# Routing product read from PSUM, row loads in quarters, line split ahead of the crosses, weight split and gate load moved

## Chip, cores and metric

The kernel runs on one core of a Trainium2 chip. The metric is the device time of one execution in microseconds, the median of several runs: 1242.65 us before the change (three runs, 1239.29 to 1244.85).

## What is computed

One transformer block on x of 32 batches x 256 tokens x 128 channels, in fp32. Six modulation vectors per batch come from c. Cut to what matters:

```
h = layernorm(x) * (1 + ca) + sa
q, k, v = h @ w_qkv.T + b_qkv                      # 16 heads of 8
write = exterior(h_prev @ w1_write.T, h @ w2_write.T)   # per head a unit 6-vector ("line")
read  = exterior(h @ w1_read.T, h @ w2_read.T)
logits = q k^T / sqrt(8) + (read . J write) * decay**(i-j) * [i>j] * bias_scale
x = x + ga * (softmax(causal logits) v @ w_out.T + b_out)
h = layernorm(x) * (1 + cb) + sb
top 2 of 8 experts by h @ Wg; weights p = softmax of the two logits
x = x + gb * sum_k p_k * ((silu(h W1[e]) * (h W2[e])) @ W3[e])
```

exterior(p1, p2) takes the six products p1[i] p2[j] - p1[j] p2[i] and divides them by their norm.

## The kernel before

**Attention stage (attend).** All engines run the same 40 iterations, b = -4 to 35, each of eight steps p = 0 to 7 (lines 101 to 104). Nothing synchronises the engines but semaphores; each has its own list of work by (b, p). In iteration b the attention of batch b is worked out, two heads per step, while the parts of other batches around it are in flight: normalisation and projections of b+3 and b+4, lines of b+2 and b+3, output projection of b-1, second norm and routing of b-2 and b-3. The small jobs that PE does between the heads stand in the table JOBS with their step, place and offset (lines 59 to 68).

A step on the engines: PE makes scores (L631 to L633) into the tile sc, incidences (L620) into inc, and for the next batch the prescores (L644 to L646) into pre; DVE weighs the incidences (L827), adds them to the scores (L794), and takes the maximum of the prescores (L806, with L811 after each four); ACT takes the exponentials (L1033); PE multiplies with the values (L660, L662). The prescores run one step less than a batch ahead: in step p of iteration b, for p from 1 on, they are those of pair p-1 of batch b+1 (lines 107 to 109).

**Rows.** fp32 numbers are cut into three bf16 parts. For the keys and queries ("dims") and for the lines, these parts are written to DRAM (kq_rows, by store_dims and store_lines: 6 and 12 DMAs by spread, L554) and read back in the layout of the scores: KT, QF, QI (load_rows, L579 to L581: three DMAs for a half of the heads). The maxima go the same way through POOL (split_peaks, L1189 to L1196), PE (L705), ACT (L1005) and a small DMA (load_peaks, L586). All these DMAs are issued by SP in one fixed order per iteration b (lines 588 to 600): peaks of b (second half), rows of b+1 (second half), store of the lines of b+2, peaks of b+1 (first half), rows of b+2 (first half), store of the dims of b+3. load_rows first holds for the stores of its batch. PE waits for the rows at the first prescores of each half (L640), so at steps 1 and 5 of an iteration.

**Lines, on POOL.** For batch b+3 at step 2: four outer products (L1236) and the cross differences (L1245, and three of L1247), then ACT squares them at step 4 (L1027), DVE sums them (L873), and at step 5 the norm is refined and applied (L1254 to L1264). For batch b+2: L1272, ACT's first part (L1061), the rest (L1128) at step 1, ACT's second part (L1064), and the last part (L1133) at step 3, behind the crosses; its end releases store_lines.

**Routing, batch b-3.** DVE marks the two chosen experts (L847, L854) at step 0. At step 2 PE's job "rank" (L738 to L741, three bf16 products) counts for each token the earlier ones with the same expert. At step 3 DVE adds the expert's base (L820, out of PSUM into slot_at), and after its maximum of the prescores it multiplies with the marks (L880, both operands in SBUF), takes the slot (L885), adds 1 to the exponential of the gap (L889), and works out the two weights (L891, L894). POOL then scatters the four token rows by indirect DMA (L1223, four per batch).

**Between the stages.** Behind its iterations ACT copies the weights' rounded parts into w_hi, which lies over the query tiles (L1112, 8 copies); DVE counts tiles per expert (L949 to L970) and subtracts to get w_lo (L974, 8 times); pads are written; then a barrier.

**Expert stage (experts).** 136 tiles of 128 tokens. SP loads a tile (L1358, up to 16 ahead), PE transposes it (L1377), multiplies up (L1384 to L1386), transposes (L1394) and multiplies down (L1402); ACT and DVE do silu, product and scaling; POOL scatters the result (L1542). ACT begins the stage with the load of gate_row (L1439, 2 MB) and a table load (L1441). The gates are used only in the last part, which adds both experts' results and x.

Of the kernel before, what the change touches and what calls it, by code (L numbers as in the profile page):

```python
# [412 lines left out]
def attend(nc, whole, stack, sb, sem, signal, v):  # L413
# [6 lines left out]
    with stack.enter_context(ExitStack()):  # L420
# [40 lines left out]
        slot_at = a("slot_at", [P, NT, E]); slot_pick = a("slot_pick", [P, NT, 2, E])  # L461
# [34 lines left out]
        rows_loaded = [signal(f"rows_loaded{n}", 48) for n in range(2)]  # L496
# [8 lines left out]
        route_step = signal("route_step", 6)  # L505
# [28 lines left out]
        with nc.Block() as block:  # L534
            @block.sync
            def _(sp):
# [33 lines left out]
                def load_rows(jb, par, half):  # L570

                    heads = slice(8 * half, 8 * half + 8)
                    hold(dims_stored, jb)
                    hold(lines_stored, jb)
                    hold(sc_ready, jb - 2, 4 * half + 4)
                    hold(inc_ready, jb - 2, 4 * half + 4)
                    hold(pre_ready, jb - 1, 4 * half + 1)
                    done = rows_loaded[half].sem
                    sp.dma_start(KT[par][0:TOP, heads, :], kq_rows[par][0, :, heads, :]).then_inc(done, 16)  # L579
                    sp.dma_start(QF[par][0:RAW0, heads, :], kq_rows[par][1, 0:RAW0, heads, :]).then_inc(done, 16)  # L580
                    sp.dma_start(QI[par][RAW0:TOP, heads, :], kq_rows[par][1, RAW0:TOP, heads, :]).then_inc(done, 16)  # L581
# [30 lines left out]
            def _(pe):  # L612
# [24 lines left out]
                def prescores(b, par, p):  # L637

                    if p % 4 == 0:
                        wait(pe, rows_loaded[p // 4], b)  # L640
# [25 lines left out]
                def job(n, b, par):  # L666
# [68 lines left out]
                    elif name == "rank":  # L735
# [4 lines left out]
                        nc.tensor.matmul(B[:, E:2 * E], onesb[:], hot_sum[:, 0, :], start=False, stop=False)  # L740
                        last = nc.tensor.matmul(B[:, 0:NT * E].rearrange("p (t e) -> p t e", t=NT), onesb[:],  # L741
# [43 lines left out]
            def _(dve):  # L785
                def body(b, par):
                    for p in range(8):
# [24 lines left out]
                        extras(b, par, p)  # L812

                def bank_copies(b, p):

                    if p == 3 and live(b - 3):
                        jb = b - 3
                        wait(dve, ready["rank"], jb)
                        B = bank[BANK["rank"]]
                        nc.vector.tensor_tensor(slot_at[:], B[:, 0:NT * E].rearrange("p (t e) -> p t e", t=NT),  # L820
                                                v["ebase"][:].unsqueeze(1).broadcast_to([P, NT, E]), ALU.add)\
                          .then_inc(used["rank"].sem, 1)
# [20 lines left out]
                def extras(b, par, p):  # L843
# [33 lines left out]
                    if p == 3 and live(b - 3):  # L877
                        jb, mine = b - 3, stage[1 - par]
                        wait(dve, used["rank"], jb)
                        nc.vector.tensor_tensor(slot_pick[:], hot[:],  # L880
                                                slot_at[:].unsqueeze(2).broadcast_to([P, NT, 2, E]), ALU.mult)\
                          .then_inc(route_step.sem, 1)
                        wait(dve, route_step, jb, 4)
# [5 lines left out]
                        nc.vector.tensor_scalar(eg1[:], egap[:], 1.0, None, ALU.add).then_inc(route_step.sem, 1)  # L889
                        wait(dve, route_step, jb, 5)  # L890
                        nc.vector.reciprocal(mine[:, :, 0, D + 1], eg1[:]).then_inc(route_step.sem, 1)  # L891
                        wait(dve, route_step, jb, 6)
# [79 lines left out]
                for e in range(E):  # L972
                    dve.wait_ge(w_high, e + 1)
                    nc.vector.tensor_tensor(w_lo[:, e, :], w_lo[:, e, :].bitcast(fp32), w_hi[:, e, :].bitcast(fp32), ALU.subtract)  # L974

            @block.scalar
            def _(act):
# [64 lines left out]
                def body(b, par):  # L1042
                    for p in range(8):
# [47 lines left out]
                        if p == 7 and live(b + 4):  # L1091
                            group = [n for n, (lo, hi) in enumerate(GROUPS) if lo <= b + 4 < hi][0]
                            wait(act, shift, group)
                            normalise(b + 4, rs1[:, b + 4], nb1[:, b + 4], xhat, ready["norm"], normed)

# [12 lines left out]
                act.wait_ge(v["w_loaded"], 16 * 3)  # L1108
                wait(act, sc_ready, NB - 1)
                wait(act, pre_ready, NB - 1)  # L1110
                for e in range(E):
# [455 lines left out]
```

## Time and profile before

| | |
|---|---|
| median of the runs | 1242.65 us |
| profiled execution | 1247.23 us, its span 1245.4 us, mean granted clock 0.963 |
| PE, DVE, ACT, POOL busy | 997, 909, 716, 815 us |
| steady attention iterations | 198 to 829 us |
| last heads to the first expert tile | 904 to 948 us |
| expert tiles, then the sum | 948 to 1202 us, to 1245 us |

A row of a timeline gives start and duration in us, engine, line, operation, output<-inputs with shapes and count, and in brackets how long the engine had idled before it and what released it. In groups of lines the figures behind the bar are busy us and the mean ns of one instruction, then the idle time before them. In tables by stretch each engine has its busy us and its count, then the granted clock of PE, the share of time in which the DMA engines were busy, and GB/s.

### The profile page before, as it was taken

How to read it: one execution, taken by the hardware profiler on the slowest of the kernel's cores; microseconds unless marked ns; L12 is line 12 of the kernel's file. 1: busy time of each engine (PE TensorE's matmuls, PEld its weight loads, DVE VectorE, ACT ScalarE, POOL GpSimd, SP SyncE). 2: the span in 40 equal slices, each digit the busy share in tenths (PEclk: the TensorE clock that was granted, in tenths of full speed). 3: DMA queues.
4: the chain of work that ended last, by engine and by line, in shares of the span. 5: the costliest groups of instructions: out<-in, count | busy, mean ns of one | idle time of the engine just before them, and what ended most of it. 6: DMA issues, size and time to landing. Idle time of an engine off the chain costs nothing. (4 is left out here: it accounts for less than half of the span.)

```text
span 1245.4 us, 30939 instructions
## 1 busy us (share of the span) xinstructions
PE 996.9 (80%) x9409; PEld 783.2 (63%) x9409; DVE 909.1 (73%) x2318; ACT 716.2 (58%) x1612; POOL 815.0 (65%) x1381
## 2 busy tenths in 40 slices
PE   2348888989898989998898989887725888888767
PEld 2236667766677767776777767766524777777653
DVE  6347888878898899889988998888644454444437
ACT  3326676767767776767776777764433444444430
POOL 6676667877787878787787878773351555555440
PEclk9999999999999999999999999999956999999988
DMA  9056565565656565656656565654113222222229
GB/s 284 29 147 161 135 163 146 157 163 133 178 139 176 142 174 146 169 149 163 158 150 167 154 165 142 176 136 130 35 43 118 77 69 73 73 74 76 67 83 352
DMA packets 206097, 170.44 MB, mean 137 GB/s; under 512 B 56944, under 2 KB 183408, under 8 KB 205808
## 3 DMA queue, kind: packets, MB, share of 16 engines
q1 hardware_dynamic: 194400, 143.21, 43.3%
q0 software_dynamic: 8704, 18.04, 4.7%
q10 hardware_dynamic: 2832, 7.20, 1.5%
q8 instruction: 81, 1.33, 0.5%
q14 instruction: 80, 0.66, 0.2%
HBM read 90.81 MB, written 76.78 MB: 135 GB/s over the span
## 5 line engine op out<-in xcount | busy, mean ns | idle before, releaser
L1033 ACT ACTIVATE PT<-sc 128x768 f32<-128x768 f32 x256 | 206.7, 807 | 234.7 <-DVE sc L794 224.8
L806 DVE TENSOR_REDUCE peak<-pre 128x6 f32<-128x768 f32 x256 | 243.6, 952 | 88.4 <-PE pre L646 82.3
L1542 POOL DMA_INDIRECT yab<-y_out,xt x136 | 131.4, 966 | 143.3 <-DVE y_out L1488 106.8
L794 DVE TENSOR_TENSOR sc<-sc,tt 128x512 f32<-128x512 f32 x256 | 176.8, 691 | 17.2 <-PE sc L633 16.1
L1223 POOL DMA_INDIRECT xg<-stage,slot_i x128 | 130.6, 1020 | 76.8 <-DVE stage L894 46.0
L827 DVE TENSOR_TENSOR tt<-inc,decay 128x512 f32<-128x512 f32 x256 | 174.2, 681 | 0.3 <-PE inc L620 0.3
L631 PE MATMUL sc<-queries,KT 128*128 128x256 bf16 x512 | 142.1, 278 | 34.5 <-ACT PT L1033 24.9
L644 PE MATMUL pre<-KT,queries 120*128 120x128 bf16 x512 | 115.7, 226 | 58.3 <-DMA QI<-kq_rows 52.8
L646 PE MATMUL pre<-causal,identb 128*128 128x256 bf16 x512 | 143.2, 280 | 0.0
L645 PE MATMUL pre<-KT,queries 120*128 120x256 bf16 x512 | 141.9, 277 | 0.0
L633 PE MATMUL sc<-identb,causal 128*128 128x256 bf16 x512 | 140.7, 275 | 0.0
L1452 ACT ACTIVATE silu<-up 128x256 f32<-128x256 f32 x136 | 52.8, 388 | 127.8 <-PE up L1386 109.2
L1495 DVE TENSOR_TENSOR hid<-silu,up 128x256 f32<-128x256 f32 x136 | 57.0, 419 | 81.0 <-ACT silu L1452 51.0
L632 PE MATMUL sc<-queries,KT 128*128 128x128 bf16 x512 | 112.9, 220 | 0.0
L644 PEld LDWEIGHTS pre<-KT,queries 120*128 120x128 bf16 x512 | 50.9, 99 | 86.6 <-DMA QI<-kq_rows 62.1
L631 PEld LDWEIGHTS sc<-queries,KT 128*128 128x128 bf16 x512 | 51.0, 100 | 77.7 <-ACT PT L1033 61.7
L620 PE MATMUL inc<-QI,KT 128*128 128x128 bf16 x1024 | 99.7, 220 | 0.1
L1236 POOL TENSOR_TENSOR outer<-lines 128x256 f32<-128x256 f32 x128 | 89.1, 726 | 5.7 <-ACT lines L997 5.7
L1402 PE MATMUL y<-w,hidT 128*128 x544 | 86.9, 284 | 2.6 <-ACT hidT L1462 1.3
L660 PE MATMUL pv<-PT,VP 128*32 128x256 f32 x1024 | 84.1, 391 | 1.5 <-ACT PT L1033 1.5
L1488 DVE TENSOR_SCALAR y_out<-y,xt 128x128 f32<-128x128 f32 x136 | 47.2, 347 | 50.1 <-PE y L1402 43.6
L1394 PE MATMUL hidT_ps<-ident,hid 128*128 128x128 f32 x272 | 55.4, 287 | 32.6 <-DVE hid L1495 30.9
(263 smaller groups left out, 2824.1 us busy)
## 6 DMA issues: line engine op xcount, KB each, us to landing
KT<-kq_rows SPq DMA_DIRECT2D x64, 480.0 KB
queries<-kq_rows SPq DMA_DIRECT2D x64, 336.0 KB
kq_rows<-dim_part SPq DMA_DIRECT2D x64, 192.0 KB, 3.0
kq_rows<-line_part SPq DMA_DIRECT2D x64, 144.0 KB
QI<-kq_rows SPq DMA_DIRECT2D x64, 144.0 KB
xt<-xg SPq DMA_DIRECT2D x136, 65.0 KB
kq_rows<-dim_part SPq DMA_DIRECT2D x64, 128.0 KB, 2.8
kq_rows<-line_part SPq DMA_DIRECT2D x64, 96.0 KB
```

What stands on the lines that cost most here:

```text
L631: nc.tensor.matmul(sc[:, n, 0:T], KT[par][:, h, 0:P], QF[par][:, h, :], start=True, stop=False)
L632: nc.tensor.matmul(sc[:, n, T:3 * P], KT[par][:, h, P:T], QF[par][:, h, P:T], start=False, stop=False)
L633: last = nc.tensor.matmul(diagonal(sc, n), causal[:], identb[:].unsqueeze(1).broadcast_to([P, 2, P]), start=False, stop=True)
L644: nc.tensor.matmul(pre[:, n, 0:P], QF[par][0:TOP, h, 0:P], KT[par][0:TOP, h, 0:P], start=True, stop=False)
L645: nc.tensor.matmul(pre[:, n, P:3 * P], QF[par][0:TOP, h, P:T], KT[par][0:TOP, h, :], start=False, stop=False)
L646: last = nc.tensor.matmul(diagonal(pre, n), identb[:], causal[:].unsqueeze(1).broadcast_to([P, 2, P]), start=False, stop=True)
L794: nc.vector.tensor_tensor(diag, diag, tt[p % 2][:], ALU.add).then_inc(added.sem, 1)
L806: nc.vector.reduce_max(peak[half][:, i:i + 2, 0:3], pre[:, :, 0:3 * P].rearrange("p n (g k) -> p n g k", g=3), AX.X)\
L827: nc.vector.tensor_tensor(tt[p % 2][:], inc[:], decay[:, 2 * p:2 * p + 2, :].unsqueeze(2).broadcast_to([P, 2, NT, P]), ALU.mult).then_inc( ...
L1033: nc.scalar.activation(PT[p % 4][:], sc[:, :, 0:3 * P], ACT.Exp).then_inc(exped.sem, 1)
L1223: nc.gpsimd.indirect_dma_start(xg[0:E * CAP, :], bass.IndirectOffsetOnAxis(slot_i[:, t, k:k + 1], 0), stage[par][:, t, k, :], None).then_i ...
L1542: nc.gpsimd.indirect_dma_start(yab, bass.IndirectOffsetOnAxis(xt[r][:, D:D + 1].bitcast(i32), 0), y_out[r % 8][:], None).then_inc(y_sent[r ...
```

## The change

1. The job "rank" gets a fourth product: the identity times the experts' bases, in fp32, added into the same PSUM bank. DVE no longer forms slot_at; it multiplies the marks with the bank directly, in the place of L820, behind a new wait for the slots of the batch before.
2. load_rows issues six DMAs for a half, three for each quarter of the heads, with a semaphore for each quarter; PE waits for a quarter at every second pair.
3. On POOL, the outer products stay at step 2; the cross differences go to step 3, behind the last part of the lines.
4. ACT's weight copies go into iteration 32, one at the end of each step; DVE's subtractions into iteration 33 likewise.
5. The gate load moves from the start of the expert stage behind tile 17.

```diff
@@ signals
-        rows_loaded = [signal(f"rows_loaded{n}", 48) for n in range(2)]
+        rows_loaded = [signal(f"rows_loaded{n}", 48) for n in range(4)]
...
-        route_step = signal("route_step", 6)
+        route_step = signal("route_step", 5)
@@ load_rows (SP)
-                    heads = slice(8 * half, 8 * half + 8)
                     hold(dims_stored, jb)
...
-                    done = rows_loaded[half].sem
-                    sp.dma_start(KT[par][0:TOP, heads, :], kq_rows[par][0, :, heads, :]).then_inc(done, 16)
-                    sp.dma_start(QF[par][0:RAW0, heads, :], kq_rows[par][1, 0:RAW0, heads, :]).then_inc(done, 16)
-                    sp.dma_start(QI[par][RAW0:TOP, heads, :], kq_rows[par][1, RAW0:TOP, heads, :]).then_inc(done, 16)
+                    for quarter in (2 * half, 2 * half + 1):
+                        heads = slice(4 * quarter, 4 * quarter + 4)
+                        done = rows_loaded[quarter].sem
+                        sp.dma_start(KT[par][0:TOP, heads, :], kq_rows[par][0, :, heads, :]).then_inc(done, 16)
+                        sp.dma_start(QF[par][0:RAW0, heads, :], kq_rows[par][1, 0:RAW0, heads, :]).then_inc(done, 16)
+                        sp.dma_start(QI[par][RAW0:TOP, heads, :], kq_rows[par][1, RAW0:TOP, heads, :]).then_inc(done, 16)
@@ prescores (PE)
-                    if p % 4 == 0:
-                        wait(pe, rows_loaded[p // 4], b)
+                    if p % 2 == 0:
+                        wait(pe, rows_loaded[p // 2], b)
@@ job rank (PE)
                         nc.tensor.matmul(B[:, E:2 * E], onesb[:], hot_sum[:, 0, :], start=False, stop=False)
+                        nc.tensor.matmul(B[:, 0:NT * E].rearrange("p (t e) -> p t e", t=NT), ident[:],
+                                         v["ebase"][:].unsqueeze(1).broadcast_to([P, NT, E]), start=False, stop=False)
@@ DVE, body and bank_copies
                         extras(b, par, p)
+                        if b == NB + 1:
+                            weights_rest(p)
+
+                def weights_rest(e):
+
+                    dve.wait_ge(w_high, e + 1)
+                    nc.vector.tensor_tensor(w_lo[:, e, :], w_lo[:, e, :].bitcast(fp32), w_hi[:, e, :].bitcast(fp32), ALU.subtract)
...
                         wait(dve, ready["rank"], jb)
+                        wait(dve, slots_ready, jb - 1)
                         B = bank[BANK["rank"]]
-                        nc.vector.tensor_tensor(slot_at[:], B[:, 0:NT * E].rearrange("p (t e) -> p t e", t=NT),
-                                                v["ebase"][:].unsqueeze(1).broadcast_to([P, NT, E]), ALU.add)\
-                          .then_inc(used["rank"].sem, 1)
+                        nc.vector.tensor_tensor(
+                            slot_pick[:], hot[:], B[:, 0:NT * E].rearrange("p (t e) -> p t e", t=NT).unsqueeze(2)
+                            .broadcast_to([P, NT, 2, E]), ALU.mult).then_inc(used["rank"].sem, 1)
@@ DVE, extras at step 3
                         wait(dve, used["rank"], jb)
-                        nc.vector.tensor_tensor(slot_pick[:], hot[:],
-                                                slot_at[:].unsqueeze(2).broadcast_to([P, NT, 2, E]), ALU.mult)\
-                          .then_inc(route_step.sem, 1)
-                        wait(dve, route_step, jb, 4)
                         wait(dve, scattered, jb - 1)
@@ DVE, behind the iterations
-                for e in range(E):
-                    dve.wait_ge(w_high, e + 1)
-                    nc.vector.tensor_tensor(w_lo[:, e, :], ..., ALU.subtract)
@@ ACT, body, and behind the iterations
+                        if b == NB:
+                            weights_first(p)
+
+                def weights_first(e):
+
+                    if e == 0:
+                        act.wait_ge(v["w_loaded"], 16 * 3)
+                        wait(act, sc_ready, NB - 1)
+                        wait(act, pre_ready, NB - 1)
+                    nc.scalar.activation(w_hi[:, e, :], w_lo[:, e, :].bitcast(fp32), ACT.Copy).then_inc(w_high, 1)
...
-                act.wait_ge(v["w_loaded"], 16 * 3)
-                wait(act, sc_ready, NB - 1)
-                wait(act, pre_ready, NB - 1)
-                for e in range(E):
-                    nc.scalar.activation(w_hi[:, e, :], w_lo[:, e, :].bitcast(fp32), ACT.Copy).then_inc(w_high, 1)
@@ POOL, body
                         if p == 2 and live(b + 3):
-                            crosses(b + 3)
+                            outer_products(b + 3)
                         if p == 3 and live(b + 2):
                             wait(pool, line_mid, b + 2)
                             nc.gpsimd.tensor_tensor(line_part[:, 2, :], line_rest[:], line_part[:, 1, :], ALU.subtract).then_inc(line_low.sem, 1)
+                        if p == 3 and live(b + 3):
+                            crosses(b + 3)
@@ experts (ACT)
-                act.dma_start(gate_row[:].rearrange("p b d -> p (b d)"),
-                              v["mod_rows"].unsqueeze(0).broadcast_to([P, NB, D])).then_inc(gates_loaded, 16)
                 nc.scalar.preload_act_table(ACT.Silu)
...
+                        if (i, r) == (1, 0):
+                            act.dma_start(gate_row[:].rearrange("p b d -> p (b d)"),
+                                          v["mod_rows"].unsqueeze(0).broadcast_to([P, NB, D])).then_inc(gates_loaded, 16)
```

## Rows read from the trace of the kernel before

**Rows 1.** Busy time by stretch, the steady attention iterations (PE, PEld, DVE, ACT, POOL).

```profile
96.00:829.00 733.00, 651.96 (x7184) 513.95 (x7183) 641.04 (x1462) 521.13 (x1055) 572.17 (x1048) 1.00 0.59 156
```

**Rows 2.** Timeline of DVE, an operation that runs once per iteration (statistics of batch b-1).

```profile
197.75 0.25 DVE L921 BATCH_NORM_AGGREGATE mv<-st 128x2 f32<-128x6 f32 x2 [0.17 <-DVE st L916]
...
400.17 0.25 DVE L921 BATCH_NORM_AGGREGATE mv<-st 128x2 f32<-128x6 f32 x2 [0.17 <-DVE st L916]
...
424.65 0.25 DVE L921 BATCH_NORM_AGGREGATE mv<-st 128x2 f32<-128x6 f32 x2 [0.17 <-issue]
...
828.53 0.25 DVE L921 BATCH_NORM_AGGREGATE mv<-st 128x2 f32<-128x6 f32 x2 [0.17 <-DVE st L916]
```

**Rows 3.** Groups by line of DVE and PE, 197.8 to 828.6 us, 25 iterations.

```profile
L889 DVE TENSOR_SCALAR eg<-egap 128x2 f32<-128x2 f32 x25 | 17.8, 713 | 0.0
L880 DVE TENSOR_TENSOR slot_pick<-hot,slot_at 128x32 f32<-128x32 f32 x25 | 17.3, 692 | 0.0
...
L820 DVE TENSOR_TENSOR slot_at<-bank,ebase 128x16 f32<-128x16 f32 x25 | 4.1, 165 | 0.0
...
L644 PE MATMUL pre<-KT,queries 120*128 120x128 bf16 x400 | 89.1, 223 | 30.8 <-DMA QI<-kq_rows 30.7
...
L746 PE MATMUL bank<-wg_sb,h2T 128*128 128x8 f32 x100 | 12.8, 236 | 0.0
```

**Rows 4.** Timelines of DVE and POOL at step 3 of iteration 16.

```profile
511.60 1.67 DVE L880 TENSOR_TENSOR slot_pick<-hot,slot_at 128x32 f32<-128x32 f32 x1
...
511.58 1.64 POOL L1133 TENSOR_TENSOR line_part<-line_rest,line_part 96x768 bf16<-96x768 f32 x1
```

**Rows 5.** The iteration from 400.3 us: waits at step 5 on DVE and PE, and busy time.

```profile
417.34 0.96 DVE L806 TENSOR_REDUCE peak<-pre 128x6 f32<-128x768 f32 x1 [0.70 <-issue]
...
416.57 0.23 PE L644 MATMUL pre<-KT,queries 120*128 120x128 bf16 x1 [1.59 <-DMA QI<-kq_rows]
...
400.30:424.90 24.60, 22.37 (x259) 17.85 (x253) 21.42 (x55) 18.31 (x38) 20.51 (x39) 1.00 0.62 164
```

**Rows 6.** SP's issues of the second half, PE behind them, and two stretches of DMA.

```profile
510.13 0.35 SPq L579 DMA_DIRECT2D KT<-kq_rows  x1
...
513.32 5.87 SPq L554 DMA_DIRECT2D kq_rows<-line_part  x12
...
516.90 0.23 PE L644 MATMUL pre<-KT,queries 120*128 120x128 bf16 x1 [0.30 <-DMA QI<-kq_rows]
...
513.25:515.50 2.25, 1.30 (x10) 0.93 (x10) 2.14 (x9) 0.71 (x2) 0.74 (x3) 1.00 0.94 248
...
517.00:521.00 4.00, 3.70 (x39) 2.88 (x42) 3.95 (x10) 2.71 (x7) 2.78 (x8) 1.00 0.55 143
```

**Rows 7.** Timeline of POOL at step 2 of iteration 16.

```profile
507.33 2.79 POOL L1236 TENSOR_TENSOR outer<-lines 128x256 f32<-128x256 f32 x4
```

**Rows 8.** The change of stage: timelines, and DMAs with KB and us to landing.

```profile
923.26 0.96 POOL L1223 DMA_INDIRECT xg<-stage,slot_i  x1 [0.30 <-issue]
...
925.62 0.19 DVE L885 TENSOR_REDUCE slot_i<-slot_pick 128x4 int32<-128x32 f32 x1 [3.41 <-DMA xg<-stage,slot_i]
...
931.69 0.96 POOL L1223 DMA_INDIRECT xg<-stage,slot_i  x1 [0.30 <-issue]
...
934.05 4.89 DVE L974 TENSOR_TENSOR w_lo<-w_lo,queries 128x512 fp32r<-128x512 f32 x8
...
948.12 0.69 PE L1377 MATMUL xT<-ident,xt 128*128 128x128 f32 x2 [23.02 <-DMA xt<-xg]
...
gate_row<-mod_rows ACTq DMA_DIRECT2D x1, 2048.0 KB, 7.6
...
wq_raw<-in_L_attn_w_qkv SPq DMA_DIRECT2D x1, 192.0 KB, 2.6
```

**Rows 9.** Timeline of ACT in iteration 32, step 2.

```profile
904.50 0.88 ACT L1101 ACTIVATE xhat<-x_all,nb,rs 128x128 f32<-128x128 f32 x2 [1.78 <-POOL nb L1180]
```

**Rows 10.** Timeline of DVE in iteration 29, step 5.

```profile
847.43 0.96 DVE L806 TENSOR_REDUCE peak<-pre 128x6 f32<-128x768 f32 x1 [2.48 <-issue]
```

More of the change, by code:

```diff
@@ L460, in attend @@
         hot = a("hot", [P, NT, 2, E]); hot_sum = a("hot_sum", [P, NT, E], bf16)
-        slot_at = a("slot_at", [P, NT, E]); slot_pick = a("slot_pick", [P, NT, 2, E])
+        slot_pick = a("slot_pick", [P, NT, 2, E])
         slot_i = a("slot_i", [P, NT, 2], i32)
@@ L889, in extras @@
                         nc.vector.tensor_scalar(eg1[:], egap[:], 1.0, None, ALU.add).then_inc(route_step.sem, 1)
+                        wait(dve, route_step, jb, 4)
+                        nc.vector.reciprocal(mine[:, :, 0, D + 1], eg1[:]).then_inc(route_step.sem, 1)
                         wait(dve, route_step, jb, 5)
-                        nc.vector.reciprocal(mine[:, :, 0, D + 1], eg1[:]).then_inc(route_step.sem, 1)
-                        wait(dve, route_step, jb, 6)
                         for t in range(NT):
@@ L971, in _ @@
                                                op0=ALU.mult, op1=ALU.add)
-                for e in range(E):
-                    dve.wait_ge(w_high, e + 1)
-                    nc.vector.tensor_tensor(w_lo[:, e, :], w_lo[:, e, :].bitcast(fp32), w_hi[:, e, :].bitcast(fp32), ALU.subtract)
             @block.scalar
@@ L1225, in scatter, with outer_products @@
                         stage[par][:, t, k, :], None).then_inc(scattered.sem, 16)
-                def crosses(jb):
+                def outer_products(jb):
                     wait(pool, used["lines"], jb)
@@ L1240, in crosses @@
                     last.then_inc(outered.sem, 1)
+                def crosses(jb):
                     wait(pool, outered, jb)
```

## The prediction

> **What bounds the kernel now.** I cut the span by stage first. The steady stretch holds most of it, and in it PE, DVE and POOL are busy for 652, 641 and 572 of 733 us [rows 1]: no engine is full, so what costs time is the loop in which they wait for each other. One operation that runs once per iteration marks the period: from 197.75 to 828.53 us it starts 26 times, so an iteration takes 630.8 / 25 = 25.23 us; but the one at 400.17 took 24.48 us [rows 2]. The reader should ask what the short ones lack.
>
> Grouping the 25 iterations by line answers it [rows 3]. Two tiny DVE operations, L880 and L889, take 17.3 and 17.8 us for 25 each, while L820, as small, takes 4.1. The excess is 13.2 + 13.7 = 26.9 us, 1.08 us per iteration. The timeline shows its nature: L880 starts 0.02 us behind POOL's L1133 and ends 0.05 us after it [rows 4]. Where L880 slips through, L889 two operations later is caught instead. L820, which reads one of its operands from PSUM and stands a step ahead, shows no long instance in its mean. The short iteration is one in which neither was.
>
> The short iteration shows the second cost [rows 5]: PE waits 1.59 us for the row load of the second half, and DVE behind it 0.70. In caught iterations this wait is partly hidden behind the stall (0.30 in one [rows 6]); over all 25, both halves together, it is 30.7 us of PE [rows 3]. So removing the stall alone brings the load wait back. **Both have to go.**
>
> The last place is the change of stage: DVE's splitting of the weights (L974, 4.89 us) is the last thing before the barrier; then a 2 MB gate load, 7.6 us to landing, is issued ahead of the first token tile, and PE's first transpose comes at 948.12 after 23 us of idling [rows 8].
>
> **The change, part by part.** The terms are for one steady iteration, from the stall-free 24.48 us.
>
> *Slot product from PSUM.* L820 goes and the product takes its place and its PSUM operand; one operation of about 0.17 us [rows 3] leaves DVE: -0.18 with its hand-over. The product should no longer be caught, as L820 is not in any of the 25. L889 still can be. It now meets a different POOL: four products (2.79 us from 507.33 [rows 7]), then the last part of the lines (1.64), then the cross differences, which lie between 510.12 and 511.58, so 1.46 us in four instructions. L880 started 4.27 us behind the first product; L889, one operation behind it, comes near 4.2 by my estimate (0.1 later than L880, 0.23 for the new PE work, some 0.4 off for the first half's load), and the last part of the lines now ends at 4.43. So I take +0.25, between 0 (it misses) and +1.6 (it comes just behind the start of L1133).
>
> *The extra fp32 product on PE.* Nearest row: fp32 pieces of 8 columns at 236 ns, of which a product has two [rows 3]; they overlap, so I take 0.23 for both, between 0.1 and 0.5. DVE waits for PE right behind, so it counts in full: +0.23.
>
> *Rows in quarters.* In rows 6 the three loads of a half are issued from 510.13 and landed by 516.90, when PE goes on: 6.8 us. The engines move 0.96 MB at about 250 GB/s, 3.9 us. If the first quarter's packets go ahead of the second's, it lands about 2 us sooner; 1.59 is needed. The second is wanted two steps, some 5 us, later. So DVE's 0.70 goes: -0.70, bounded by 0 and by -1.2, the mean of PE's waits (30.7 / 25). The price is three more issues per half on SP, at 0.49 us (twelve in 5.87) 1.5 us, 3 us an iteration. SP's next work behind the second half is the store of the lines, issued at 513.32 when L1133 ended at 513.22: SP sat idle. Six issues end by 510.13 + 2.9 = 513.1, and L1133 now ends 1.46 us sooner, so the store starts a little sooner, not later. Behind the first half the store of the dims waits for POOL anyway. Three extra issues are hidden: 0.
>
> *Lines ahead of the crosses.* Besides the above: the differences end 5.9 us behind the first product, 1.64 later than now. ACT's square waits for them, and DVE's norm behind it. Between L889 (4.2 by the estimate above) and the square lie two small operations, L794 and the exponential, some 2 us: 6.2. Slack 0.3: 0, at worst +0.4. The new wait for the slots of the batch before is a whole iteration old: 0.
>
> Sum: 24.48 - 0.18 + 0.25 + 0.23 - 0.70 = 24.08, 1.15 below the mean. **Steady: 25 x 1.15 = -28.8.** PE was busy 22.37 us in that iteration [rows 5] and gets 0.23 more, so 1.5 us of room is left. Four first iterations wait alike but are hardly caught: 4 x 0.75 = -3. Of the two iterations before the last, one has a DVE wait of 2.48 us behind the load [rows 10]; the other three loads of the two are late by less, some 0.6 us each by estimate from rows 5: -3.5 of 4.3. The start-up gets the lines out 1.46 us sooner and the crosses 1.64 later: -1, from -4 to +2.
>
> *Weights split early.* DVE's 4.89 leaves the end. What is late next: the last scatter is issued until 932.65, and its predecessors landed about 1.4 us behind issue, so 934.1; DVE's own last small operation also ends at 934.1 [rows 8]. Gain 4.8. The cover for the work: ACT's eight copies of 0.6 us go one after each step of the iteration behind the last batch; ACT idled 1.78 before L1101 [rows 9] and most others fit into such gaps; the one before L1009 doesn't: +0.6. DVE's eight (0.61 each) fall where it waits, but the first three stand beside POOL's variance chain, on the path. L974 reads two SBUF tiles as L880 does; if POOL loses turns, +1, between 0 and +2. The trace shows only DVE blocked by POOL, never the reverse. The Trainium skill ("SBUF — State Buffer", Who interferes with whom) says that whoever starts first holds the shared port for the whole instruction, so POOL would wait up to 0.67 us each time; by it I would add 2 where the sum has 1.
>
> *Gates at tile 17.* The first tile, issued some 0.3 us behind the gates, lands with them, 7.3 us behind its own issue; a small load in an empty queue takes 2.6 us (w_qkv, 192 KB) [rows 8]: -4.7, at least -3. Behind tile 17 the 2 MB share the engines with the tiles, but these are loaded up to 16 ahead: 0, at worst +2. **Transition: -4.8 - 4.7 + 0.6 + 1 = -7.9.**
>
> **Total:** -28.8 - 3 - 3.5 - 1 - 7.9 = -44.2. The profiled execution took 1247.2 us (span 1245.4), so it would take 1203; it stood 4.6 us above the median of 1242.65, and I forecast 1199 against that.
>
> **Rivals.**
> *A, the first quarter lands no sooner* (the packets of both are moved side by side). The stall goes, the load wait stays as in the short iteration: 24.48 + 0.30 = 24.8 per iteration, -11 in the steady stretch; with the transition and -2 elsewhere, -21: 1222. For it: no row shows in which order the packets of two loads are moved. Against: the queue is one and the loads are issued in turn.
> *B, another wait takes over.* DVE, PE and POOL form one loop; ACT's square behind the crosses, or L889 caught for longer, takes half the gain: 0.6 per iteration, -15, others -13: 1215. For: PE's 1.5 us of room; L889 near the edge. Against: POOL idles 5.5 us an iteration [rows 1].
> *C, slower: packets half as long cost as much each.* Place: the row loads on SP's queue. A half then needs 3.9 us more; the first quarter lands as now, the store of the lines queues behind it, and the next half load, which holds for those lines, goes out some 2 to 3 us late, so PE waits that much there: about +1.5 per iteration net, +38, less 16 elsewhere: 1264. It decides from the point where a 2 KB packet takes over some 1.4 times its share. Against: in rows 6 packets of 4 KB move 248 GB/s at a share of 0.94 (264 at full), the 512 and 256 byte ones of the stores 143 at 0.55 (260). The Trainium skill ("DMA: Bandwidth & Descriptors", Bandwidth) asks for transfers of 1 MB for 75% of the peak; halving 480 KB goes against it, and by it this rival would be likelier than I make it.
> *D, no change:* the stall moves to L889 in full (1.6 in place of 0.25): 25.43 per iteration, +5; the rest gives -8, with POOL's chain blocked by its bound: 1240.
>
> **Numbers.** Forecast 0.62, A 0.14, B 0.15, C 0.04, D 0.05. The forecast's own range is a period of 23.6 to 24.5 and the bounds of the rest: 1186 to 1215; A reaches to 1228. Range 1186 to 1226. A measurement here can tell 0.5% (6 us). Faster: forecast, A, B less a little: 0.90; same 0.06; slower 0.04.
>
> **What would show it.** L880's line without long instances; L889's mean under 0.45 us against 0.713; PE's wait for rows under 5 us in the 25 iterations against 30.7; period 23.9 to 24.3. SP's store of lines starts 2.4 to 3.1 us behind the first row load's issue, 3.2 now. The weights' subtraction is gone from the end, and PE's first transpose comes about 7 us behind the last scatter's start, 16.4 now. Wrong if the period stays above 24.8, or the row waits stay.

## The result, and the profile after

| | before | after |
|---|---|---|
| median of the runs shown | 1242.35 us (1239.29 to 1244.85, 4 runs) | 1179.8 us (1178.28 to 1181.02, 4 runs) |
| profiled execution, its span | 1247.23, 1245.4 us | 1179.46, 1177.7 us |
| ratio, 95% interval | | 0.9497, 0.9473 to 0.9521 |

The changed kernel is 62.6 us faster by the medians. The ratios in this document use fast runs alone: two runs of f2 (1254.76 and 1255.42 us) and two of e6 (1910.83 and 4165.69 us, whose length nothing here explains) are left out. I had forecast 1199 (1186 to 1226), a gain of 44: the direction is right, the size is too small, and the time lies outside the range. The table cuts both spans at the same places and sets the forecast's terms beside them.

| stage, us | before | after | change | forecast |
|---|---|---|---|---|
| to DVE's first addition to the scores | 95.9 | 94.3 | -1.7 | -1 |
| iterations 0 to 3 | 101.8 | 91.9 | -9.9 | -3 |
| 25 steady iterations (4 to 28) | 630.8 | 593.4 | -37.4 | -28.8 |
| iterations 29 and 30 | 53.1 | 45.7 | -7.3 | -3.5 |
| iteration 31, to DVE's last addition to the scores | 18.0 | 19.2 | +1.2 | 0 |
| from there to the start of the last scatter | 32.1 | 34.2 | +2.1 | +1.6 |
| to PE's first transpose | 16.4 | 7.6 | -8.8 | -9.5 |
| expert tiles and the sum | 297.3 | 291.4 | -5.9 | 0 |
| all (rounded) | 1245.4 | 1177.7 | -67.7 | -44.2 |

The last line but one can't be credited to the change: seven experiments that left this stage alone took 280 to 291 us for it, and before's 297 was the longest of all. On the two chips that had both kinds, 289 to 291 us without the later gate load stand against 290 to 296 with it, so a cost of some 2 us by it isn't excluded. Without that line the difference is 61.8, close to what the medians say.

Busy time by stretch, the kernel after (columns as in [rows 1]); the rows are iterations 0 to 3, 4 to 28, and 29 and 30, cut up to 0.3 us later than in the table:

```profile
94.25:186.30 92.05, 84.40 (x953) 67.32 (x957) 80.41 (x160) 67.49 (x131) 65.35 (x121) 1.00 0.55 163
186.30:779.90 593.60, 563.12 (x6286) 448.81 (x6279) 540.11 (x1278) 454.82 (x925) 505.64 (x928) 1.00 0.57 168
779.90:825.60 45.70, 39.45 (x474) 31.03 (x467) 41.16 (x99) 24.39 (x46) 20.37 (x43) 1.00 0.44 131
```

PE is now busy for 563 of 593.6 us of the steady stretch. The same iterations before held 563.78 us of PE's work in 630.50. The work did not shrink; the idling did. Timeline of DVE, the operation of [rows 2]:

```profile
186.14 0.25 DVE L929 BATCH_NORM_AGGREGATE mv<-st 128x2 f32<-128x6 f32 x2 [0.17 <-issue]
...
779.58 0.25 DVE L929 BATCH_NORM_AGGREGATE mv<-st 128x2 f32<-128x6 f32 x2 [0.17 <-issue]
```

Period: 593.44 / 25 = 23.74 us, 25.23 before. Groups by line of the 25 iterations, against [rows 3] (L645 was L644, L897 was L889, L831 is the product that was L880):

```profile
L645 PE MATMUL pre<-KT,queries 120*128 120x128 bf16 x400 | 88.7, 222 | 1.5 <-DMA QI<-kq_rows 0.8 <-issue 0.7
...
L897 DVE TENSOR_SCALAR eg<-egap 128x2 f32<-128x2 f32 x25 | 16.2, 648 | 0.0
L831 DVE TENSOR_TENSOR slot_pick<-hot,bank 128x32 f32<-128x32 f32 x25 | 4.4, 177 | 0.0
```

PE's wait for the rows fell from 30.8 us to 1.5. The product from PSUM is 177 ns all 25 times. But L897 is still caught, all 25 times: 648 ns on average where a free one takes 158. So one of the two stalls is half there, and the kernel is faster than I said. That is the first sign that the stall was not what I took it for. POOL and SP in iteration 4:

```profile
193.26 2.79 POOL L1248 TENSOR_TENSOR outer<-lines 128x256 f32<-128x256 f32 x4
196.00 1.65 POOL L1143 TENSOR_TENSOR line_part<-line_rest,line_part 96x768 bf16<-96x768 f32 x1
...
195.43 0.34 SPq L580 DMA_DIRECT2D KT<-kq_rows  x1
...
198.23 5.91 SPq L554 DMA_DIRECT2D kq_rows<-line_part  x12
```

```profile
197.14 0.53 DVE L897 TENSOR_SCALAR eg<-egap 128x2 f32<-128x2 f32 x1
```

L897 starts 3.88 us behind the first outer product (about 4.2 forecast) and ends with L1143 (at 197.65), the wait for it that the forecast had; SP's store of the lines starts 2.80 us behind the first issue of the row load (forecast 2.4 to 3.1). At the change of stage (timelines of POOL and PE):

```profile
878.64 0.97 POOL L1235 DMA_INDIRECT xg<-stage,slot_i  x1 [0.30 <-issue]
...
886.28 0.47 PE L1392 MATMUL xT<-ident,xt 128*128 128x128 f32 x1 [14.26 <-DMA xt<-xg]
```

7.64 us from the last scatter to the first transpose, "about 7" forecast.

### The profile page after: what moved, and what is told of

Read it like the earlier page. It is cut to its first block and busy times, and to the rows that moved or that the text cites. A ratio compares the mean times of both kernels' runs of the same rounds, so it can differ in the third digit from the quotient of the medians.

```text
span 1177.7 us, 31322 instructions
## 1 busy us (share of the span) xinstructions
PE 990.3 (84%) x9473; PEld 783.4 (67%) x9473; DVE 887.4 (75%) x2286; ACT 717.9 (61%) x1612; POOL 815.6 (69%) x1381
## 5 line engine op out<-in xcount | busy, mean ns | idle before, releaser
L809 DVE TENSOR_REDUCE peak<-pre 128x6 f32<-128x768 f32 x256 | 243.5, 951 | 47.7 <-PE pre L647 47.1
L1235 POOL DMA_INDIRECT xg<-stage,slot_i x128 | 131.0, 1023 | 62.6 <-issue 42.5
L632 PE MATMUL sc<-queries,KT 128*128 128x256 bf16 x512 | 141.3, 276 | 17.6 <-ACT PT L1038 11.5
L645 PE MATMUL pre<-KT,queries 120*128 120x128 bf16 x512 | 114.5, 224 | 9.1 <-DVE peak L809 5.7
L1504 DVE TENSOR_SCALAR y_out<-y,xt 128x128 f32<-128x128 f32 x136 | 47.2, 347 | 56.8 <-PE y L1417 45.7
L621 PEld LDWEIGHTS inc<-QI,KT 128*128 128x128 bf16 x1024 | 78.8, 98 | 3.2 <-DVE tt L839 0.3
L1409 PE MATMUL hidT_ps<-ident,hid 128*128 128x128 f32 x272 | 54.7, 283 | 26.9 <-DVE hid L1511 22.8
```

The lines of the kernel that those rows point to most:

```text
L621: last = nc.tensor.matmul(inc[:, n, t, :], KT[par][:, h, blk], QI[par][:, h, blk], start=True, stop=True)
L632: nc.tensor.matmul(sc[:, n, 0:T], KT[par][:, h, 0:P], QF[par][:, h, :], start=True, stop=False)
L809: nc.vector.reduce_max(peak[half][:, i:i + 2, 0:3], pre[:, :, 0:3 * P].rearrange("p n (g k) -> p n g k", g=3), AX.X)\
L1235: nc.gpsimd.indirect_dma_start(xg[0:E * CAP, :], bass.IndirectOffsetOnAxis(slot_i[:, t, k:k + 1], 0), stage[par][:, t, k, :], None).then_i ...
```

## The experiments

**Theory 1**: the row load, the stall and POOL's order are one knot. A late load holds PE and DVE up until DVE's small operations meet POOL's long one; the stall fills time in which the next load would have been waited for anyway. The quarters alone carry the gain. **Theory 2**, the forecast's: the stall (1.08 us an iteration) and the load wait (0.70) are costs of their own, and both have to go.

All results, with the period of the 25 iterations, PE's wait for rows in them, the time of the two DVE operations that can be caught (8.1 to 8.5 us for 50 free ones), and the number of stretches within them in which PE's granted clock is 0.50. Before is the first trace, and ratios are to runs of before on the same chip.

| kernel | ratio, 95% | period | PE waits for rows | the two on DVE | half-clock stretches |
|---|---|---|---|---|---|
| before | 1 | 25.23 | 30.8 | 35.1 | 0 |
| after | 0.9497 (.9473-.9521) | 23.74 | 1.5 | 20.6 | 0 |
| e1 quarters | 0.9512 (.9467-.9557) | 23.69 | 1.2 | 9.7 | 0 |
| e2 PSUM product | 0.9994 (.9962-1.0025) | 25.38 | 35.8 | 33.9 | 2 |
| e3 order | 1.0059 (1.0023-1.0095) | 25.57 | 46.2 | 21.9 | 3 |
| e4 PSUM, quarters | no interval; 1178.38 us | 23.79 | 1.6 | 11.3 | 0 |
| e5 gates | 0.9953 (.9929-.9978) | 25.40 | 31.4 | 35.1 | 1 |
| e6 weights | 0.9996 (.9971-1.0022) | 25.29 | 25.6 | 41.0 | 0 |
| e7 changed | 0.9467 (.9437-.9496) | 23.73 | 0.0 | 20.2 | 0 |
| e8 all but quarters | 1.0054 (1.0018-1.0089) | 26.08 | 53.9 | 15.5 | 8 |
| f1 first quarter held | 0.9833 (.9783-.9883) | 24.77 | 25.5 | 24.6 | 1 |
| f2 nothing to catch | 1.0003 (.9971-1.0036) | 25.70 | 50.6 | 8.1 | 6 |
| f3 quarters, gates | 0.9491 (.9448-.9535) | 23.65 | 1.2 | 10.6 | 0 |
| f4 quarters, gates, weights | 0.9500 (.9461-.9539) | 23.60 | 0.5 | 10.0 | 0 |

**Quarters alone.**

```diff
-                    heads = slice(8 * half, 8 * half + 8)
+                    for quarter in (2 * half, 2 * half + 1):
+                        heads = slice(4 * quarter, 4 * quarter + 4)
...
-                        wait(pe, rows_loaded[p // 4], b)
+                        wait(pe, rows_loaded[p // 2], b)
```

> Only the row loads in quarters, all else as before. Theory 1 (the stall is a consequence of the load wait: without some 0.4 us of wait at step 1 DVE reaches L880 and L889 before POOL starts the last part of the lines): the two operations are hardly caught, L889's and L880's means fall near 0.2 us, the period falls to about 23.8 us, the time to about 1202 us. Theory 2 (separate costs, as the prediction had it: both have to go): the stall of about 1.1 us stays, only part of the load wait comes back as time, the period stays at 24.6 to 24.9, the time 1225 to 1232.

Median 1173.51 us against 1231.35. Groups by line of its 25 iterations (one line number further down than before):

```profile
L645 PE MATMUL pre<-KT,queries 120*128 120x128 bf16 x400 | 88.8, 222 | 1.2 <-DMA QI<-kq_rows 0.8 <-issue 0.3
...
L881 DVE TENSOR_TENSOR slot_pick<-hot,slot_at 128x32 f32<-128x32 f32 x25 | 5.7, 227 | 0.0
...
L890 DVE TENSOR_SCALAR eg<-egap 128x2 f32<-128x2 f32 x25 | 4.0, 158 | 0.0
```

Nothing was done about the stall here, and it is gone: with the rows there in time DVE reaches L881 and L890 before or just as POOL starts its long operation, which begins 4.23 to 4.30 us behind the first product; L890 starts 3.63 to 4.26 us behind it, and its longest instance is 0.16 us. This one part gives the whole steady gain. Theory 2's separate costs fall here.

**Slot product from PSUM alone, and the order on POOL alone.**

```diff
-                                slot_at[:].unsqueeze(2).broadcast_to([P, NT, 2, E]), ALU.mult)
+                            slot_pick[:], hot[:], B[:, 0:NT * E].rearrange("p (t e) -> p t e", t=NT).unsqueeze(2)
```

```diff
-                            crosses(b + 3)
+                            outer_products(b + 3)
...
+                        if p == 3 and live(b + 3):
+                            crosses(b + 3)
```

> Only the slot product from PSUM with the fourth rank product. Both theories: L880 can't be caught, but L889 comes just behind the start of the last part of the lines and is caught in most iterations for 1.2 to 1.6 us, and the load wait stays. Theory 1: period 24.9 to 25.3, time within 8 us of before. Theory 2 with L889 escaping half the time: period 24.7, time 1229.

> Only the last part of the lines ahead of the crosses. Theory 1: L880 now comes near the end of the last part of the lines (0.2 us of stall) or behind the first cross difference (up to 0.6), the load wait stays as in the stall-free iterations of before (PE 1.6 us at step 5): period 24.6 to 24.8, time 1227 to 1232. Theory 2 (the order only moves the stall from one POOL instruction to the next): period 25.1, time as before within 4 us.

Groups by line, e2 and then e3:

```profile
L644 PE MATMUL pre<-KT,queries 120*128 120x128 bf16 x400 | 89.6, 224 | 35.8 <-DMA QI<-kq_rows 35.8
...
L889 DVE TENSOR_SCALAR eg<-egap 128x2 f32<-128x2 f32 x25 | 29.5, 1180 | 0.0
L823 DVE TENSOR_TENSOR slot_pick<-hot,bank 128x32 f32<-128x32 f32 x25 | 4.4, 177 | 0.0
```

```profile
L644 PE MATMUL pre<-KT,queries 120*128 120x128 bf16 x400 | 89.5, 224 | 46.2 <-DMA QI<-kq_rows 45.7 <-DVE peak L806 0.4
...
L880 DVE TENSOR_TENSOR slot_pick<-hot,slot_at 128x32 f32<-128x32 f32 x25 | 13.5, 541 | 0.0
L889 DVE TENSOR_SCALAR eg<-egap 128x2 f32<-128x2 f32 x25 | 8.4, 338 | 0.0
```

In e2 the stall only moves on to L889. In e3 it shrinks from 35.1 to 21.9 us for the two, and PE's wait for the rows grows from 30.8 to 46.2: what one gives, the other takes. Both theories for e3 missed: the period was to be 24.6 to 24.8 or 25.1 and is 25.57, three half-clock stretches among it, and the ratio, 1.0059, is clear of 1 on the slow side. In before, e2, e3, e5, e6 and e8 the two columns add up to 66 to 70 us each time, in f2 to 59.

**PSUM product and quarters.** Two of the edits together, run once beside before's 1231.35 us.

```diff
+                        done = rows_loaded[quarter].sem
...
+                            slot_pick[:], hot[:], B[:, 0:NT * E].rearrange("p (t e) -> p t e", t=NT).unsqueeze(2)
```

> Product from PSUM and quarters, POOL's order as before. Theory 1: L889 stands at 4.1 to 4.2 us behind the first outer product, the last part of the lines starts at 4.24: it escapes in most iterations and is caught for 1.5 us in some; period 23.6 to 24.2, time 1197 to 1210. Theory 2: the sum of the single gains of e1 and e2.

Period 23.79 against 23.69 for quarters alone: no gain by the PSUM product shows beside them.

**The parts at the end.** Gates alone, weights alone, then the changed kernel (e7, no edit) and the change without its quarters (e8), all beside the same runs of before. The edits of e5, of e6, and what e8 takes back of the change:

```diff
+                        if (i, r) == (1, 0):
+                            act.dma_start(gate_row[:].rearrange("p b d -> p (b d)"),
```

```diff
+                        if b == NB + 1:
+                            weights_rest(p)
...
+                        if b == NB:
+                            weights_first(p)
```

```diff
-                    for quarter in (2 * half, 2 * half + 1):
+                    heads = slice(8 * half, 8 * half + 8)
```

> Only the gate load behind tile 17. From the last scatter's start to PE's first transpose 16.4 us now; the barrier stays where it is (DVE's subtractions), the first tile lands some 3.5 us behind its issue in place of 7.3: 12.6 us, and nothing is lost behind tile 17: time 4 us below before (ratio 0.997). If the 2 MB delay the tiles in the middle of the stage by as much as they did in front, the ratio is 1.000.

> Only the weights split in iterations 32 and 33. Scatter to transpose 16.4 us now, 11.6 without the 4.9 us of DVE; but from the last scores to the last scatter some 2 us more than 32.1, as ACT's and DVE's pieces stand in the chain of the last batch, or POOL waits for DVE's port: net 2 to 3 us below before (ratio 0.998). If all pieces fall into idle time, 4.8 us below (0.996).

> The changed kernel, on the chip of these runs. If quarters alone carry the steady part (e1 gave a ratio of 0.951), the ratio is 0.943 to 0.948: e1's less 7 us of transition. If the other parts cost in the steady stretch what they bring at the end, it is 0.950 as in the first measurement.

> The whole change but the quarters. Theory 1 (the load wait makes the loop): steady period 24.6 to 25.0, PE waits 1.5 us for rows at step 5, L889 caught for 0.4 us; with some 7 us off at the end 1215 to 1225 where before is 1231 to 1242. Theory 2 (the stall has its own price): the stall is gone for the most part, so period 24.3, ratio 0.975.

Gates: 10.92 us from the last scatter to the first transpose (16.4 before), -5.5, where the forecast had -4.7; the time is 0.47% less. Weights: 12.99, so -3.4 there, but from the last scores to the last scatter 34.06 in place of 32.09: 2.0 are paid back, and the ratio shows nothing. That pay-back has a place. Timelines of POOL in the iteration of the weights, of the kernel after, and of f3, which has no early weights:

```profile
859.95 0.79 POOL L1186 TENSOR_SCALAR ve<-mv 128x2 f32<-128x2 f32 x1 [2.56 <-DVE mv L929]
860.81 0.51 POOL L1187 TENSOR_SCALAR nm<-mv 128x2 f32<-128x2 f32 x1
861.41 1.02 POOL L1190 TENSOR_TENSOR rs<-ve,neg_half 128x2 f32<-128x2 f32 x1
```

```profile
857.91 0.23 POOL L1175 TENSOR_SCALAR ve<-mv 128x2 f32<-128x2 f32 x1 [2.04 <-DVE mv L922]
858.22 0.22 POOL L1176 TENSOR_SCALAR nm<-mv 128x2 f32<-128x2 f32 x1
858.53 0.72 POOL L1179 TENSOR_TENSOR rs<-ve,neg_half 128x2 f32<-128x2 f32 x1
```

Beside them, on DVE of the kernel after:

```profile
859.96 1.89 DVE L822 TENSOR_TENSOR w_lo<-w_lo,queries 128x512 fp32r<-128x512 f32 x3
```

POOL's three small operations now start while DVE's three long ones run: 0.79 + 0.51 + 1.02 against 0.23 + 0.22 + 0.72, so 1.15 us more, on the chain that ends in the last scatter. e6 shows the same 0.79, 0.51 and 1.02. This is the stall of [rows 4] with the roles exchanged. By the Trainium skill ("SBUF — State Buffer", SBUF: two separate sides) whichever of the two starts first has the shared port pair for the whole instruction. The rows agree in that POOL's first two end 0.1 us behind one of DVE's three; whether DVE's first one did start first they can't tell, as it stands at 859.96 and POOL's at 859.95.

The changed kernel gives 0.9467 on this chip, inside the 0.943 to 0.948 of quarters as the sole steady part. The change without its quarters is 0.5% slower than before, and neither theory had that: theory 1 had put its period at 24.6 to 25.0, and it is 26.08. PE waits 53.9 us for the rows, and its clock falls. Groups by line, then busy time in three stretches:

```profile
L644 PE MATMUL pre<-KT,queries 120*128 120x128 bf16 x400 | 90.0, 225 | 53.9 <-DMA QI<-kq_rows 53.8
...
L896 DVE TENSOR_SCALAR eg<-egap 128x2 f32<-128x2 f32 x25 | 11.1, 444 | 0.0
```

```profile
445.00:448.40 3.40, 1.60 (x19) 1.40 (x17) 2.60 (x6) 2.95 (x8) 2.79 (x7) 1.00 1.04 281
448.40:451.80 3.40, 3.40 (x26) 2.55 (x29) 2.31 (x6) 1.16 (x2) 3.09 (x6) 0.50 0.21 52
451.80:455.20 3.40, 3.40 (x45) 3.07 (x46) 1.49 (x8) 0.51 (x2) 2.43 (x4) 1.00 0.27 36
```

PE was busy 1.60 of 3.40 us, and then the granted clock is 0.50 (the 1.2 GHz level) for the next 3.40, in which it ends 26 matmuls where the stretch after has 45. There are 8 such stretches in the 25 iterations, none in those of before and none in those of any kernel whose quarters are free.

**The first quarter held back.** Six loads a half as in e1, but steps 1 and 5 wait for both quarters.

```diff
                         wait(pe, rows_loaded[p // 2], b)
+                    if p % 4 == 0:
+                        wait(pe, rows_loaded[p // 2 + 1], b)
```

> The quarters alone, as in the run before that took 0.951 of the time, but TensorE waits at steps 1 and 5 for both quarters of the half, not for the first. Same number and size of loads, same order on SP. Theory 1 (the gain is that the first quarter lands some 2 us before the half does, so that nobody is late): the gain is gone, period 25.0 to 25.6, ratio to before 0.99 to 1.01, PE idle 0.5 to 2 us ahead of the prescores of steps 1 and 5 and L880 or L889 caught again in most iterations. Rival (the shorter transfers by themselves disturb less, or land sooner as a whole): period under 24.3, ratio under 0.97.

Neither: 0.9833, period 24.77, between the two. Of the 1.54 us that quarters gain per iteration 1.08 go with the early first quarter, and 0.46 stay; of the 4.9% of the time, 1.7% stay. Groups by line:

```profile
L647 PE MATMUL pre<-KT,queries 120*128 120x128 bf16 x400 | 88.7, 222 | 25.5 <-issue 25.2
...
L883 DVE TENSOR_TENSOR slot_pick<-hot,slot_at 128x32 f32<-128x32 f32 x25 | 18.1, 724 | 0.0
```

The semaphore records of the DMAs (some are missing, so these are lower bounds) say why. For the second half of an iteration, counted from the first issue of its load, the last record of the whole half comes at 6.85 us in before (median of 25) and 6.02 in f1; the first quarter's at 4.25. (For the first half of an iteration the three are 7.04, 6.65 and 4.72.) So quarters bring the first heads 2.3 to 2.6 us sooner and the whole half 0.4 to 0.8 sooner. Why six smaller loads end sooner than three larger ones no run here shows; PE's wait at step 5 fits it, mostly 0.5 to 1.0 in f1 and 1.5 to 1.75 in before's iterations in which nothing was caught.

**Nothing left to catch.** Half loads as before; the product from PSUM, and the addition made a sum over a pair that holds 1.0 in its second place.

```diff
-                        nc.vector.tensor_scalar(eg1[:], egap[:], 1.0, None, ALU.add).then_inc(route_step.sem, 1)
+                        nc.vector.reduce_sum(eg1[:], egap[:], AX.X).then_inc(route_step.sem, 1)
```

> The kernel before with the slot product from PSUM alone, and L889's addition of 1 made as a sum over a pair (the second of the two holds 1.0), a form of DVE instruction that was never long in any trace of this case. So neither of the two operations that were caught can be, while the half loads stay. Theory 1 (the stall only takes up time that DVE would spend waiting for the late load): no gain, period 25.0 to 25.5, ratio 0.995 to 1.005, and PE's wait for the rows grows from 1.2 us an iteration towards 1.6 or more. Theory 2 (the stall costs 1.08 us of its own, less what the load takes back, as rival A of the prediction had it): period 24.5 to 24.8, ratio 0.985 to 0.99. If the addition is still long (over 0.4 us), the run tells nothing on this.

Groups by line:

```profile
L808 DVE TENSOR_REDUCE peak<-pre 128x6 f32<-128x768 f32 x200 | 190.6, 953 | 74.6 <-PE pre L646 56.8 <-issue 17.6
L644 PE MATMUL pre<-KT,queries 120*128 120x128 bf16 x400 | 90.1, 225 | 50.6 <-DMA QI<-kq_rows 49.4 <-DVE peak L808 0.9
...
L889 DVE TENSOR_REDUCE eg<-egap 128x2 f32<-128x4 f32 x25 | 3.7, 147 | 0.0
```

The experiment does what it should: 147 ns each time, 27 us less in the two operations than before. And the time is the same, 1.0003, period 25.70. DVE waits 24 us longer for PE (74.6; 50.5 in before), and PE 20 longer for the rows; six half-clock stretches come on top. One could say that the clock took back what the lost stall gave; but the 19 iterations without such a stretch average 25.26 us, against 25.23 in before. So with half loads the stall cost nothing: the late load stood behind it. Theory 1 holds for what costs the time, with two amendments: a third of the quarters' gain stays when the first quarter is held back, which fits the whole half landing sooner but isn't tied to it by any run (f1), and where the load wait is left alone, less stall comes with more half-clock stretches (e3, e8, f2), and twice with a time 0.5 to 0.6% longer (e3, e8).

**What is needed of the change.** Two of its five parts, then three.

f3 has the edits of e1 and e5, f4 those and e6's:

```diff
+                        if (i, r) == (1, 0):
+                            act.dma_start(gate_row[:].rearrange("p b d -> p (b d)"),
```

```diff
+                        if b == NB:
+                            weights_first(p)
```

> Two of the five parts: rows in quarters and gates at tile 17. Theory 1 (quarters carry the steady gain, the slot product from PSUM and the order of lines and crosses add nothing beside them): period 23.6 to 23.8, last scatter to first transpose 9 to 11 us, ratio 0.944 to 0.949, the same as the whole change (0.9467) within what can be told. Theory 2 (each part has its share): the whole change is at least 5 us ahead of this one, ratio here 0.951 or more.

> Three of the five parts: quarters, gates, weights split early. Theory 1: period 23.6 to 23.8, last scatter to first transpose 7.5 to 8.5 us, but the last iterations some 2 us longer, so that it stands within 2 us of the run with quarters and gates alone: ratio 0.943 to 0.949. Theory 2: 0.95 or more, the whole change at 0.9467 ahead of it by what the slot product and the order bring.

Medians 1178.77 and 1181.18 us, ratios 0.9491 and 0.9500; the changed kernel had 0.9467 on its second chip and 0.9497 on its first. Within the intervals the three are one. (f4's 0.9500 touches what theory 2 had for it, but its period is the shortest of all; what it lost is in the expert tiles, 296 us against 290 in f3.) From the last scatter to the first transpose they take 11.02, 8.31 and 7.8 us, and from the last scores to the last scatter 32.07, 34.06 and 34.16. So the product from PSUM, the order of lines and crosses and the weights leave no difference that could be measured beside quarters and gates. No version here beat the changed kernel clearly.

## Why the prediction was wrong

**The step that failed is the split of the steady loop into a stall of 1.08 us and a load wait of 0.70**, with the conclusion "Both have to go". I subtracted L880 and L889 from the period because their excess (26.9 us) matched what the short iteration lacked. The one short iteration of [rows 2], 24.48 us, was no fair base. Four of the 25 are free of the stall and take 24.51 us on average. Two more are held for 0.5 and 0.4 us only, and they are the longest of all. The timeline of DVE before has one of them:

```profile
272.84 0.25 DVE L921 BATCH_NORM_AGGREGATE mv<-st 128x2 f32<-128x6 f32 x2 [0.17 <-DVE st L916]
...
285.76 0.57 DVE L880 TENSOR_TENSOR slot_pick<-hot,slot_at 128x32 f32<-128x32 f32 x1
...
286.46 0.16 DVE L889 TENSOR_SCALAR eg<-egap 128x2 f32<-128x2 f32 x1
...
300.11 0.25 DVE L921 BATCH_NORM_AGGREGATE mv<-st 128x2 f32<-128x6 f32 x2 [0.17 <-DVE st L916]
```

It takes 27.27 us, the other 26.04, with PE waiting 3.0 us for rows in each. The six average 25.23 us, and so do the 19 that are caught in full; PE waits 2.12 us for rows in the former, 0.95 in the latter. So the profile before already hinted that the stall was free. It was a correlation: an iteration without a wait at step 1 was short and let DVE slip past POOL. e1 removes the load wait alone and both vanish (23.69); f2 removes the stall alone and nothing does (25.70). The sentence beside it, that removing the stall alone brings the load wait back, was right, and more so than I priced it: rival A had 24.8 us for that state, f2 measured 25.70 and e8 26.08. This wrong split did not put the time outside the range: as the change removed both parts at once, their sum is right whichever of them carries it, and that is luck. Two mis-sized groups of terms did it, which follow.

**The steady sum came out 0.34 too high**, 24.08 against 23.74, 8.6 us over 25 iterations. The core of it, 24.48 - 0.70 = 23.78, is what quarters alone gave (23.69). The three further terms, +0.30 together, add nothing that shows: the product is 177 ns (0.17 forecast), L897's excess 0.49 (0.25 forecast, 1.6 at most), and the third, the new fp32 product on PE, is two pieces of 263 ns. DVE still waits 28.0 us for PE in 25 iterations (at L809), which could cover them; that it does is argued, not shown. Here e4, e7, f3 and f4, with periods of 23.60 to 23.79, tell no part from another.

**Iterations 0 to 3, 29 and 30 were the largest miss by proportion**: -17.2 against -6.5. "Four first iterations wait alike but are hardly caught: 4 x 0.75" took the steady wait for granted. The waits view of before says otherwise, first from 96 to 198 us, then from 828 to 882 (engine and line, what it waited for, us, times, longest):

```profile
PE pre L644 <- DMA QI<-kq_rows: 9.8, 7, 2.6
...
PE pre L644 <- DMA QI<-kq_rows: 7.8, 4, 2.4
```

17.6 us of PE's wait in six iterations, 2.9 each, against 1.2 in a steady one; the kernel after has none there. The gain, 17.2, looks like the same sum, but it isn't. Busy time by stretch before, the same iterations:

```profile
95.94:197.75 101.81, 87.48 (x961) 70.17 (x962) 82.16 (x160) 67.49 (x131) 65.94 (x123) 0.97 0.57 148
828.53:881.59 53.06, 42.30 (x478) 33.11 (x470) 41.89 (x100) 24.11 (x47) 20.50 (x43) 0.94 0.43 116
```

PE idles 11 us less after the change and is busy 6 us less (129.8 before, 123.9 after). Before, the granted clock fell to 0.50 there four times for 3.4 us, at 112.4, 187.5, 846.3 and 873.6 us; after, not once. The forecast had no term for the clock at all. That the quarters did it is shown by repetition: the six traces with quarters free took 91.5 to 93.1 us for iterations 0 to 3 and 44.9 to 47.4 for 29 and 30, the seven with half loads 97.9 to 102.9 and 50.8 to 53.6. I had one row of this, 2.48 us on DVE [rows 10], and gave its neighbours 0.6 by analogy where the waits of these stretches would have told.

**The transition was right within about 1 us.** To the first transpose -8.8 (-9.5 forecast), pay-back by the weights +2.1 (+1.6), so -6.7 against -7.9. Iteration 31 became 1.2 longer, which I had at 0; the other kernels took 17.3 to 19.5 us for it, with and without the parts of the change, so this may be chance. The bound "between 0 and +2" for POOL losing turns held: 1.15 in the variance chain, with 1 in the sum.

**The rivals.** A's premise is refuted (the first quarter's last record comes at 4.25 us, 2.6 sooner; about 2 forecast). B did not come: no wait took over. C's premise too: twice as many packets half as long took no longer as a whole, 6.02 against 6.85 us. The Trainium skill ("DMA: Bandwidth & Descriptors", Bandwidth) asks for transfers of 1 MB or more for at least 75% of the peak; halving loads of 480 KB and less made the kernel faster all the same (e1, 0.9512), as what it waited for most was the first heads of a load. Of D, L897 is caught, but for 0.49 us and not 1.6, and at no cost that shows.

The range failed although the steady period, 23.74, is inside its bounds of 23.6 to 24.5: the two short groups of iterations alone hold 10.7 of the 18.6 us that were missed, and the time lies 6.2 below the lower end.

## What to carry to other kernels

When a wait and a stall share a loop, their traces do not say which is the cost: subtracting the busy time of a stalled instruction is a forecast of its removal only if nothing is late behind it. Look for what is late at the *start* of the loop, shorten that first (here: let the consumer of a large load wait for its first piece), and see whether the stall is left. Before taking one stall-free iteration as the base, put all that have little stall beside it. And read the waits and the clock of the first and last iterations on their own: here they waited more than twice as long as the steady ones.

## What the runs showed of the hardware

A stall between DVE and POOL goes both ways: DVE's operations of 0.16 to 0.18 us took up to 1.7 behind POOL's 1.64 us one [rows 4], and POOL's 0.23 us one took 0.79 behind DVE's. A sum over a pair in SBUF (147 ns) did not stall in any of 25 iterations in a place where the addition of a constant to as many elements took 1180 ns on average.

Waiting has a second price that the forecast did not have. With half loads PE's granted clock fell to 0.50 for 3.4 us at a time (once in e2 for 6.8): within the 25 steady iterations 8 times in e8, 6 in f2, 3 in e3, 2 in e2, once each in e5 and f1, never in before. Outside them, in iterations 0 to 3 and 29 and 30, it fell in every kernel with half loads, before among them, and in none with quarters free, but for up to 3.4 us at the very start of iteration 0. The steady iterations that it falls in are 26.4 to 28.5 us long. The others average 25.26 in f2, level with before, and 25.54 in e8; why e8's are longer stays open. Which pattern of idling sets the clock off was not tried and stays open too.
